# A transformer decoder on one core: where ScalarE rounds a piece of feed-forward weights within an attention unit

## What is computed

```python
x = x + _L0_attn_ref(_layernorm(x, axis=-1), L0_attn_W_Q, L0_attn_W_K, L0_attn_W_V, L0_attn_W_O)
x = x + _L0_xattn_ref(_layernorm(x, axis=-1), ctx_1024, ctx_1024, mask_BxS2_bk1, ...)
x = x + _L0_ffn_ref(_layernorm(x, axis=-1), L0_ffn_wqkv, ..., L0_ffn_w1, L0_ffn_b1, L0_ffn_w2, L0_ffn_b2)
...
scores = jnp.einsum('bach,baCh->bacC', k, q)
causal = jnp.tril(jnp.ones((n, n), dtype=bool))
masked = jnp.where(causal, scores, jnp.float32(-MASK_VAL))
attn = jax.nn.softmax(masked / np.float32(np.sqrt(D_HEAD)), axis=-1)
z = jnp.einsum('bacC,baCh->bach', attn, v)
out = jnp.einsum('aeh,bach->bce', W_O, z)
```

## Time and profile before

| | us |
|---|---|
| median of 3 runs | 1173.26 |
| lowest and highest of the 3 | 1170.98, 1173.38 |
| time of the profiled execution | 1168.97 |
| its span, first to last instruction | 1167.2 |
| stage with the pieces | 92 to 337 |

### The profile page before, as it was taken

How to read it: one execution, slowest core, us unless ns; L and a number is a source line. 1 busy time by engine, 2 the same in 40 slices (tenths; PEclk the granted TensorE clock), 3 DMA queues, 4 the chain that set the end, 5 groups by cost and what they waited for, 6 DMA issues and landing times.

```text
span 1167.2 us, 20315 instructions
## 1 busy us (share of the span) xinstructions
PE 1130.6 (97%) x6858; PEld 895.0 (77%) x6858; DVE 837.8 (72%) x2481; ACT 705.8 (60%) x1742; POOL 612.8 (53%) x641
## 2 busy tenths in 40 slices
PE   8899999999999999999989999999999999999987
PEld 6778787888787877676667787887878878777676
DVE  6788787878788655769886767768666677684553
ACT  3578777778776513453566756546656476575822
POOL 1455657565655311229886546547456465573420
PEclk9899999999999999999999999999999999999999
DMA  8124545554532501021021000300002100001011
GB/s 270 37 56 132 172 125 170 148 172 125 164 113 73 181 19 55 1 95 37 19 113 62 1 1 1 127 1 2 1 20 97 55 1 1 1 7 67 1 38 35
DMA packets 40549, 81.48 MB, mean 70 GB/s; under 512 B 5888, under 2 KB 18304, under 8 KB 39936
## 3 DMA queue, kind: packets, MB, share of 16 engines
q1 hardware_dynamic: 40448, 80.20, 22.0%
HBM read 41.04 MB, written 22.36 MB: 54 GB/s over the span
## 4 chain that ended last, share of the span: by engine, by line
PE 86%; DVE 6%; ACT 5%; issue 2%; POOL 1%; DMA 0%; SPq 0%; DVEq 0%; ACTq 0%; POOLq 0%
PE psum L1551 52%; PE psum L1649 6%; PE psum L1631 5%; PE psum L1781 5%; PE psum L1830 5%; PE psum L1797 4%; PE psum L1815 4%; PE psum L1763 2%; ACT probs L909 1%; DVE probs L1156 1%; ACT lp L993 1%; PE psum L1558 1%; PE psum L1737 1%; PE psum L1854 1%; PE psum L1843 1%
## 5 line engine op out<-in xcount | busy, mean ns | idle before, releaser
L751 POOL TENSOR_TENSOR probs<-probs,rden 128x128 f32<-128x128 f32 (+3 forms) x256 | 178.3, 728 | 80.8 <-DVE rden L1168 80.8
L993 ACT ACTIVATE lp<-lp,lneg,rn 128x256 f32<-128x256 f32 (+1 forms) x256 | 143.6, 568 | 17.3 <-DVE lneg L1385 17.2
L909 ACT ACTIVATE probs<-probs,negmax 128x128 f32<-128x128 f32 (+3 forms) x256 | 140.8, 552 | 11.5 <-DVE negmax L1163 10.9
L1156 DVE CUSTOM_DVE_ANT_0 probs<-psum,causal 128x512 f32<-128x512 f32 (+3 forms) x256 | 109.9, 485 | 16.2 <-PE psum L1551 16.0
L784 POOL TENSOR_TENSOR lp<-lp,lrden 128x128 f32<-128x128 f32 x64 | 25.6, 400 | 176.0 <-DVE lrden L1390 176.0
L796 POOL TENSOR_TENSOR rn<-ssm,neg_half 128x8 f32<-128x8 f32 x64 | 108.1, 1690 | 0.0
L1373 DVE CUSTOM_DVE_ANT_0 lp<-psum,local 128x256 f32<-128x256 f32 (+1 forms) x256 | 84.2, 385 | 20.6 <-PE psum L1781 20.6
L787 POOL TENSOR_TENSOR lp<-lp,lrden 128x768 f32<-128x768 f32 x64 | 93.9, 1467 | 0.0
L980 ACT ACTIVATE sq<-psum 128x512 f32<-128x512 f32 x64 | 37.8, 594 | 86.8 <-PE psum L1551 82.1
L874 ACT ACTIVATE pT<-psum 128x512 f32<-128x512 f32 (+1 forms) x96 | 46.9, 517 | 67.9 <-PE psum L1631 67.8
L1631 PE MATMUL psum<-ident,probs 128*128 128x128 f32 x640 | 86.1, 274 | 1.2 <-POOL probs L751 1.2
(11 more groups left out here) (172 smaller groups left out, 3244.7 us busy)
## 6 DMA issues: line engine op xcount, KB each, us to landing
k<-k_round SPq DMA_DIRECT2D x128, 128.0 KB, 2.4
w_raw<-in_w_all SPq DMA_DIRECT2D x22, 380.0 KB, 3.9
w_scratch<-w_half SPq DMA_DIRECT2D x22, 380.0 KB, 4.3
w_scratch<-w_rest SPq DMA_DIRECT2D x22, 380.0 KB, 4.6
x<-in_x SPq DMA_DIRECT2D x8, 512.0 KB, 6.0
aw<-in_w_quads SPq DMA_DIRECT2D x4, 768.0 KB, 5.3
wqkv_lo<-w_scratch SPq DMA_DIRECT2D x6, 512.0 KB, 6.5
wqkv_hi<-w_scratch SPq DMA_DIRECT2D x6, 512.0 KB, 4.5
```

Source lines behind the costliest of these rows:

```text
L751: ins = pool.tensor_tensor(pr, pr, rden[:, u % 2, h, i:i + 1].broadcast_to([P, TRI[i]]), ALU.mult)
L909: ins = act.activation(pr, pr, ACT.Exp, bias=negmax[:, u % 2, h, i:i + 1], scale=ADH ** -0.5, accum_out=den[:, u % 2, h, i:i + 1])
L993: ins = act.activation(pr, pr, ACT.Exp, bias=lneg[:, u % 2, h, w:w + 1], scale=rn[:, m % 2, w, 0, 2 * j + h:2 * j + h + 1], accum_out=lden ...
L1156: ins = dve.tensor_tensor_reduce(probs[:, u % 2, h, TRI_AT[i]:TRI_AT[i + 1]], bank[:, at:at + TRI[i]], causal[:, S - TRI[i]:S], 1.0, -3e38 ...
```

## The change

In ScalarE's repeated list the token `part` moves from behind `pk@2` to behind `e1@1`:

```diff
-        UNIT_ACT = ("t1 e0@1 pk@2 part t3 t5 aw0 pq@2 aw1 e1@1 pv@2 aw2")
+        UNIT_ACT = ("t1 e0@1 pk@2 t3 t5 aw0 pq@2 aw1 e1@1 part pv@2 aw2")
```

## The result

| | before | changed |
|---|---|---|
| median | 1172.12 us (6 runs) | 1299.74 us (6 runs) |
| lowest, highest | 1170.59, 1173.38 | 1299.34, 1302.28 |
| span of the profiled execution | 1167.2 | 1300.5 |

The ratio is 1.1092, with a 95% interval of 1.108 to 1.1104. The forecast was 1305 us, from 132 us on top of before; 127.6 us came.

What follows compares the result with a forecast made beforehand. TensorE, busy 97% of the span, was taken as the bound. To the median of 1173.26 us came 92 for stalls behind GpSimd's queue and 40 for clock falls: 1305 us, range 1263 to 1335.

Steps and rivals of the forecast that it cites:

- The rest holds the factors, 18 times, 5.13 us each: 92 us: GpSimd makes head 0's factors behind the later rest, so TensorE starts 5.13 us later at 18 pieces: 92 us.
- The loop is closed: The chain through TensorE, ScalarE and GpSimd returns to the next `t0`, so a unit takes 16.6 us against 11.5.
- The clock falls in each stall, 2.2 us each: 40 us: TensorE's granted clock falls in each of 18 stalls, priced between 1.8 and 2.7 us, taken as 2.2: 40 us.
- Four pieces in the start list lose 0.4 us each: Pieces 0, 1, 3 and 4, between both heads' factors on GpSimd, delay `t3` some 0.4 us each, 1.6 in all.
- SyncE's stores cost nothing: On SyncE the later stores of a piece still go out ahead of the next transfers of k, costing nothing.
- The gain is at most 1.1 us: On ScalarE the copies of `t3` and `t5` may start earlier, saving at most 1.1 us of waits by `z`.
- GpSimd does not take a later instruction first: GpSimd keeps strict order, against the rival that TensorE's work hides the move: 1170 to 1173 us, chance 0.02.
- The upper end of the range: Top of the forecast range, 1335 us, said to take in a third more than the row's clock loss of 2.7 us.

## Why the prediction was right

- **The rest holds the factors, 18 times, 5.13 us each: 92 us.** Right. The trace has 18 stalls of 5.0 to 5.5 us; with the clock held full the units are 16.73 us long against 16.62 forecast. Taking the factors of head 0 out from behind the rest gives 125 us back, with ScalarE's list untouched.
- **The loop is closed.** Right. Nine stalls cost half of 18, and a rounding placed 2.2 us earlier makes each unit 2.2 us shorter (14.53 against 16.73, both at full clock).
- **The clock falls in each stall, 2.2 us each: 40 us.** Right in kind, a little too large. It fell at each of the 18, none of the 16 intervals between the first `t0` of units 10 and 26 is under 18.1 us, and the kernel with the stalls filled is 32 us faster. Over these intervals the changed kernel takes 300.6 us (168.25 to 468.88) and the filled one 268.6 (168.11 to 436.69): 2.0 us each, 36 for 18. The price of 2.7 from one row of before is the upper of the two values that occur. That the middle of 1.8 and 2.7 came near is in part luck, for the reason given for the lower value was wrong: a fall early in the stall, I had reasoned, leaves less work at half rate and costs 1.8. It was the other way round. The falls that came 0.9 to 1.9 us before TensorE began cost 2.7, with 6.8 us at half level, and those that came about when it began 1.6, with 3.4 us. That stretches of two lengths take turns I had not foreseen, and no run here shows why they do.
- **Four pieces in the start list lose 0.4 us each.** Wrong in size. One of them cost 0.95 us, at `t3` of unit 6 behind the `aw` steps, and the others nothing that shows. I added rounding and rest to the present start of the factors (225.84), but the rounding would start 0.4 us ahead of that, at 225.46, so they end 5.1 and not 5.5 us into the unit, exactly when they are needed. The kernel with every rest between the factors confirms the smaller figure. It changed the sum by nothing, as the gain from the copies cancelled it.
- **SyncE's stores cost nothing.** Right for this kernel, and for the reason given: in the unit shown the stores go out at 203.16 and 203.52, ahead of the next unit's k at 214.52. Where the rest starts 2.65 us into the next unit (219.07 less 216.42, scaling on ScalarE) and not 4.5 us ahead of it, the cover is gone: TensorE waited 6.6 us for k, most of it where the load of attention weights went out between the stores and k as well.
- **The gain is at most 1.1 us.** Nothing contradicts it: in the stretch of the changed kernel TensorE waits for nothing but the factors. That the freed copies can be worth more is suggested only by the two kernels with the rest behind both heads, 6.4 us apart; no run isolates it there, since their rests do not fall at the same times.
- **GpSimd does not take a later instruction first.** Right, but the row was misread. Of the 4.06 us that it stood idle in the earlier trace rows the reciprocal was ready only for the last 0.7 (from 220.38 on, rows 7). The changed kernel shows it far better: 6.4 us idle with the reciprocal ready, from 194.93 to 201.35.
- **The upper end of the range.** A third more than the row's loss gives 1330 us (1173 + 92 + 65), not 1335. Nothing hangs on it.

The sum by the measured terms: 92 for the stalls, 36 for the clock, 1 for the unit behind `aw` steps and less 1.1 for the copies, 128 us. In the traces the time from `t0` of unit 4 to `t0` of unit 27 grows from 268.1 to 397.0 us, by 128.8. The medians differ by 127.6. The two profiled executions differ by 133.3, for the one of before was 3.2 us below its median and the changed one 2.5 above; 4.2 us of that lie behind unit 27, where both kernels do the same.

## What to carry to other kernels

When a step moves on one engine, look up who waits for its result, and then what is queued behind that waiter: here 0.8 us of rounding that nobody needs soon held up, through a subtraction that nobody needs soon either, the one product that the busiest engine wanted next. If the chain returns to the same engine within an iteration, its delay is paid in every iteration, and each stall of TensorE of 2.5 to 5 us may cost 1.6 to 2.7 us more through the clock. The remedy is to order the waiter's queue by when each result is needed, and to check that a long GpSimd instruction then doesn't run beside short VectorE ones on the critical path.

## What the hardware showed beyond that

- A 128 x 4 scaling on VectorE took up to 1.8 us instead of 0.17, and ended 0.01 to 0.04 us behind a GpSimd subtraction of 1.83 us that it had met (20 cases). Against GpSimd's factors, whose instructions are shorter, it took 0.41 or 0.42 (16 cases).
- TensorE's clock fell at seven of 15 stalls of 2.85 us, in the case shown about 1 us after work had begun again, and at all stalls of 5.0. It fell as well behind waits of 2.41, 2.52 and 2.78 us, and not behind the one of 3.0 us. So the length of the stall alone does not decide it.
- Between units 10 and 26 the stalls of 5 us, alike in length, cost 1.6 and 2.7 us by turns, with the clock at half level for 3.4 and for 6.8 us.
- Filling stalls of 5 us with 18 useless products kept the clock at 1.00 and made the kernel 32 us faster.
